# Token rows of the experts: indirect transfers through memory in place of one-hot products

## The reference

```python
logits = flat_x @ gate_w.T                        # 16 experts
scores = softmax(logits, axis=-1).T
topk_weight, topk_idx = top_k(scores, C)          # each expert takes its 74 best tokens
xg = flat_x[topk_idx]                             # [16, 74, 256]
g = einsum('ecd,eid->eci', xg, Wg)                # 1024 hidden
u = einsum('ecd,eid->eci', xg, Wu)
h = gelu(g) * u
eo = einsum('eci,edi->ecd', h, Wd) * topk_weight[..., None]
flat_out = zeros_like(flat_x).at[topk_idx.reshape(-1)].add(eo.reshape(-1, d))
out = flat_out + gelu(x @ Sg.T) * (x @ Su.T) @ Sd.T     # shared expert
```

## Time and profile before

| | |
|---|---|
| median of 3 runs | 814.61 us (814.48 to 814.78) |
| the profiled execution | 815.38 us, span 813.6 us |
| PE busy | 794.0 us, 98% |
| DVE busy | 632.2 us, 78% |
| ACT busy | 460.1 us, 57% |
| POOL busy | 251.7 us, 31% |
| moved by DMA | 88.36 MB, queue q1 busy 30.8% of 16 engines |

### The profile page before, as it was taken

The page is one execution under the profiler, slowest core; times in us unless marked ns, Lnnn a source line. Parts: engine busy times, 40 slices in busy tenths (PEclk is TensorE's granted clock), DMA queues, the critical chain, the costliest instruction groups (busy, mean ns, idle before and its releaser), DMA issues.

```text
span 813.6 us, 16629 instructions
## 1 busy us (share of the span) xinstructions
PE 794.0 (98%) x6060; PEld 744.2 (91%) x6060; DVE 632.2 (78%) x1287; ACT 460.1 (57%) x829; POOL 251.7 (31%) x297
## 2 busy tenths in 40 slices
PE   9999999999999999999999999999999999999988
PEld 8898789999999999898999999899998999999758
DVE  5796684778778776778797877878778787876796
ACT  3486424433333336585786778677687767745421
POOL 0012120410111100364366147336624623643020
PEclk9999999999999999999999999999999999999999
DMA  6010946998888822010210031031012103020001
GB/s 192 1 53 1 382 137 243 329 330 309 308 336 309 325 62 108 1 40 15 93 51 0 13 103 39 13 103 39 3 38 75 39 13 103 23 86 1 1 0 31
DMA packets 18290, 88.36 MB, mean 109 GB/s; under 512 B 3120, under 2 KB 7472, under 8 KB 12240
## 3 DMA queue, kind: packets, MB, share of 16 engines
q1 hardware_dynamic: 18256, 87.90, 30.8%
HBM read 85.05 MB, written 2.84 MB: 108 GB/s over the span
## 4 chain that ended last, share of the span: by engine, by line
PE 47%; issue 23%; POOL 18%; DVE 8%; ACT 3%; POOLq 0%; DVEq 0%; ACTq 0%
PE bank L1151 14%; POOL W_L L2017 7%; PE bank L1188 6%; POOL HF_L L2075 4%; POOL arena L1998 3%; PE bank L731 3%; POOL WQKV_L L2017 3%; PE bank L883 2%; PE bank L1197 2%; PE bank L1061 2%; PE bank L756 2%; PE bank L916 1%; PE bank L799 1%; POOL SQ L2036 1%; PE bank L1135 1%
## 5 line engine op out<-in xcount | busy, mean ns | idle before, releaser
L1151 PE MATMUL bank<-arena 128*128 (+1 forms) x1024 | 117.8, 274 | 0.0
L1151 PEld LDWEIGHTS bank<-arena 128*128 128x128 f32 x1024 | 117.4, 192 | 0.0
L1998 POOL TENSOR_TENSOR arena<-arena,srec 111x456 f32<-111x456 f32 x56 | 52.3, 961 | 123.8 <-DVE srec L2171 123.8
L2017 POOL TENSOR_TENSOR W_L<-LW,W_H 128x256 fp32r<-128x256 f32 x96 | 68.6, 751 | 35.4 <-DVE XHL L2609 32.1
L2075 POOL TENSOR_TENSOR HF_L<-arena,HF_H 128x296 fp32r<-128x296 f32 x48 | 43.8, 936 | 75.6 <-ACT HF_H L1913 75.6
L799 PE MATMUL bank<-XHL,W_H 128*128 128x296 f32 x288 | 64.8, 306 | 0.0
L1913 ACT ACTIVATE arena<-bank,vec 128x296 f32<-128x296 f32 x96 | 48.8, 509 | 20.8 <-PE bank L799 15.0
L2029 POOL TENSOR_TENSOR QW<-QW,arena x14 | 22.4, 1600 | 119.0 <-DVE QW L2510 65.6
L1342 PE MATMUL bank<-HF_L,W_H 128*128 128x296 f32 x192 | 57.4, 299 | 0.0
L1342 PE MATMUL bank<-HF_H,W_H 128*128 128x296 f32 x192 | 57.4, 299 | 0.0
L1342 PE MATMUL bank<-HF_H,W_L 128*128 128x296 f32 x192 | 57.3, 299 | 0.0
(11 more groups left out here) (276 smaller groups left out, 2183.4 us busy)
## 6 DMA issues: line engine op xcount, KB each, us to landing
arena<-ew_in SPq DMA_DIRECT2D x16, 2048.0 KB, 9.2
arena<-ew_in SPq DMA_DIRECT2D x16, 1024.0 KB, 6.9
LW<-lw_in SPq DMA_DIRECT2D x12, 1024.0 KB, 5.0
arena<-route SPq DMA_DIRECT2D x32, 185.0 KB, 3.3
LW<-lw_in SPq DMA_DIRECT2D x6, 768.0 KB, 4.4
fp_weights<-arena SPq DMA_DIRECT2D x1, 2048.0 KB, 6.4
arena<-fp_weights SPq DMA_DIRECT2D x1, 2048.0 KB, 7.3
arena<-patches_in SPq DMA_DIRECT2D x2, 864.0 KB, 8.3
```

What stands on the lines that cost most here:

```text
L1151: last = mm(o[:, m * CAP:(m + 1) * CAP], w[:, kc, mi * P:(mi + 1) * P], xg(kc, e), start=(kc == 0), stop=(kc == C - 1))
L1998: nc.gpsimd.tensor_tensor(v, v, srec[0:QROWS, s:s + 2, :].unsqueeze(3).to_broadcast([QROWS, 2, C * JH, KEYS]), ALU.mult).then_inc(p_ready, 1)
L2017: last = nc.gpsimd.tensor_tensor(low[:, cols], value[:, cols], high[:, cols], ALU.subtract)
```

## The change

Two tables in memory are new: `rows_in`, where SP stores the turned tokens together with their 16 scores (272 numbers a row), and `rows_out`, which POOL fills with zeros. Only experts 0 and 1 are still gathered by one-hot products, and only expert 15 is scattered by them. The rows of experts 0 and 1 are fetched by indirect transfers too, for their scores alone. Otherwise:

- DVE sums, for every slot, the numbers of the tokens in it (`expert_slots`) and turns them into integers. POOL fetches the 74 rows of `rows_in` by these numbers with an indirect transfer (`gather`), two experts ahead; PE turns them (`turn_gathered`, two transposes between down(e) and up(e+1)), and ACT copies them into one of two places in `XG`.
- DVE keeps token numbers and weights of the running expert (`keep_slots`), ACT scales its output (`EOT`), and POOL adds the 74 rows into `rows_out` by an indirect transfer that adds (`scatter`). Ahead of each indirect transfer POOL executes a one-element addition (`step`).
- At the end SP loads `rows_out`, and PE adds it into the banks by products with the identity (`add_rows`). The shared expert's result is added to `H` before the first expert.
- SP loads gate and up in transfers of their own (1 MB each), gate earlier than before, and one routing row in place of two.
- POOL's `split_weights("qkv", 0)` moves behind its loop.

```diff
-            def load_gate_up(e, s):
-                sp.dma_start(EW[s][:, 0:EGU_N], a["ew"][e][:, 0:EGU_N]).then_inc(ld_gu[s], 16)
+            def load_gate(e, s):
+                sp.dma_start(EW[s][:, 0:C * EI], a["ew"][e][:, 0:C * EI]).then_inc(ld_gu[s], 16)
+
+            def load_up(e, s):
+                sp.dma_start(EW[s][:, C * EI:EGU_N], a["ew"][e][:, C * EI:EGU_N]).then_inc(ld_up[s], 16)
...
+            by_tile = rows_in.rearrange("(t p) n -> p t n", p=P)
+            sp.wait_ge(moe_dve, MOE_DVE["probs"])
+            sp.dma_start(by_tile[:, :, D:GW], lg[:, 2]).then_inc(rows_stored, 16)
+            sp.wait_ge(moe_act, MOE_ACT["ut4"])
+            sp.dma_start(by_tile[:, :, 0:D], UT).then_inc(rows_stored, 16)
...
-            with sp.Fori(1, E // 2) as i:
+
+            def load_expert(i, s):
+
+                e2 = i * 4 + (2 * s - 4)
+                sp.wait_ge(u_psum, e2 + 2)
+                load_up(i * 2 + s, s)
+                sp.wait_ge(slot_summed, i * 2 + (s - 1))
+                load_route(i * 2 + s, s)
+                if not isinstance(i, int) or 2 * i + s < E - 1:
+                    sp.wait_ge(g_psum, e2 + 4)
+                    load_gate(i * 2 + (s + 1), 1 - s)
+                sp.wait_ge(d_psum, i * 2 + (s - 1))
+                load_down(i * 2 + s, s)
+
+            sp.wait_ge(g_psum, 2)
+            load_gate(2, 0)
+            with sp.Fori(1, E // 2 - 1) as i:
                 for s in range(2):
-
-
-                    sp.wait_ge(u_psum, i * 4 + (2 * s - 2))
-                    load_gate_up(i * 2 + s, s)
-                    sp.wait_ge(sw_ready, i * 2 + (s - 1))
-                    load_route(i * 2 + s, s)
-                    sp.wait_ge(d_psum, i * 2 + (s - 1))
-                    load_down(i * 2 + s, s)
+                    load_expert(i, s)
+            for s in range(2):
+                load_expert(E // 2 - 1, s)
+
+            sp.wait_ge(scattered, landed(E - 2))
+            sp.dma_start(TL, rows_out.rearrange("(t p) n -> p t n", p=P)).then_inc(ld_rows, 16)
...
-            for q in range(4):
-                pe.wait_ge(moe_dve, MOE_DVE[f"onehot{q}"])
-                for c in range(C):
-                    i = 2 * q + c
-                    if i >= 4:
-                        pe.wait_ge(moe_act, MOE_ACT[f"xg{i - 4}"])
-                    for t in range(NT):
-                        for part in (UT_H, UT_L):
-                            last = mm(bank[i % 4][:, 0:4 * CAP], part[:, t, c * P:(c + 1) * P],
-                                      OH[:, q % OH_RING, t, :, :].rearrange("p e s -> p (e s)"),
-                                      start=(t == 0 and part is UT_H), stop=(t == NT - 1 and part is UT_L))
-                    mark(last, f"xg{i}")
+            pe.wait_ge(moe_dve, MOE_DVE["onehot"])
+            for c in range(C):
+                for t in range(NT):
+                    for part in (UT_H, UT_L):
+                        last = mm(bank[2 + c][:, 0:2 * CAP], part[:, t, c * P:(c + 1) * P],
+                                  OH[:, t, :, :].rearrange("p e s -> p (e s)"),
+                                  start=(t == 0 and part is UT_H), stop=(t == NT - 1 and part is UT_L))
+                mark(last, f"xg{c}")
...
+            def turn_gathered(e, s):
+
+                if s == 0:
+                    pe.wait_ge(moe_dve, MOE_DVE["shared_added"])
+                pe.wait_ge(gathered[s], group(e) * 16 + 32)
+                pe.wait_ge(xg_ready, plus(e, 2))
+                for c in range(C):
+                    at = c * CAP
+                    last = nc.tensor.transpose(bank[5][:, at:at + CAP], G[0:CAP, s, c * P:(c + 1) * P], ident[0:CAP, 0:CAP])
+                last.then_inc(xg_turned, 1)
+
+            def add_rows():
+
+                pe.wait_ge(ld_rows, 16)
+                for c, t0, n, bk, col, opens in ACC:
+                    for t in range(NT):
+                        lo, hi = max(t0, t * P), min(t0 + n, (t + 1) * P)
+                        if lo < hi:
+                            mm(bank[bk][:, col + lo - t0:col + hi - t0], TL[:, t, c * P:(c + 1) * P],
+                               ident[:, lo - t * P:hi - t * P], start=(opens and lo == t0), stop=False,
+                               skip_group_check=True)
+
...
             def expert_step(e, s, nxt, ns):
 
-                if nxt is not None:
-                    gate_free(nxt)
-                    expert_up(nxt, ns, 0)
+                gate_free(nxt)
+                expert_up(nxt, ns, 0)
                 expert_down(e, s)
-                if nxt is not None:
-                    up_free(nxt)
-                    expert_up(nxt, ns, 1)
-                expert_scatter(e)
-
...
+            turn_weights(0, GROUPS_DOWN - 1)
+            add_rows()
+            turn_weights(GROUPS_DOWN - 1, GROUPS_DOWN)
+            last_scatter()
...
+            def expert_out(e1, s):
                 act.wait_ge(d_psum, e1 + 1)
-                act.wait_ge(sw_ready, e1 + 1)
-                if not (isinstance(e1, int) and e1 == 0):
-                    act.wait_ge(scat_done, e1)
-
-                f(EOT_H[0:CAP, :], bank[4][0:CAP, 0:D], ACT.Copy, scale=wslot[0:CAP, :]).then_inc(eot_ready, 1)
...
+            def gathered_out(e1, s):
+
+                act.wait_ge(xg_turned, e1 + 1)
+                f(XG[:, :, s, :], bank[5][:, 0:C * CAP].rearrange("p (c n) -> p c n", c=C), ACT.Copy
+                  ).then_inc(xg_ready, 1)
...
-            split_weights("qkv", 0)
+
+            def step(n):
+
+                if not (isinstance(n, int) and n == 0):
+                    pool.wait_ge(pool_stepped, n)
+                nc.gpsimd.tensor_tensor(pool_step[:, :], zero1[:, :], zero1[:, :], ALU.add).then_inc(pool_stepped, 1)
+
+            def gather(e, s, n):
+
+                pool.wait_ge(slot_ready, e + 1)
+                step(n)
+                pool.wait_ge(rows_stored, 32)
+                nc.gpsimd.indirect_dma_start(G[0:CAP, s, :], None, rows_in[:, :],
+                                             bass.IndirectOffsetOnAxis(ap=slot_id_i[0:CAP, s:s + 1], axis=0)
+                                             ).then_inc(gathered[s], 16)
+
+            def scatter(e, s, n):
+
+                pool.wait_ge(eot_ready, e + 1)
+                pool.wait_ge(scattered, landed(e, 0))
+                step(n)
+                pool.wait_ge(rows_stored, 32)
+                nc.gpsimd.indirect_dma_start(rows_out[:, :], bass.IndirectOffsetOnAxis(ap=scatter_id[0:CAP, s:s + 1], axis=0),
+                                             EOT[0:CAP, :], None, compute_op=ALU.add).then_inc(scattered, 16)
+
+            gather(0, 0, 0)
+            gather(1, 1, 1)
             with pool.Fori(0, QSLICES) as i:
-                for k, ready, done in ((1, w_scaled, w_divided), (0, w_rounded, w_quantised)):
+                for s, k, ready, done in ((0, 1, w_scaled, w_divided), (1, 0, w_rounded, w_quantised)):
+                    gather(i * 2 + (s + 2), s, i * 4 + (2 * s + 2))
+                    scatter(i * 2 + s, s, i * 4 + (2 * s + 3))
                     pool.wait_ge(ready, i + 1)
                     nc.gpsimd.tensor_tensor(QW_slice[:, i, :, :], QW_slice[:, i, :, :],
                                             qscale[:, i, k, :].unsqueeze(2).to_broadcast([P, QBLOCKS, FP4_BLOCK]),
                                             ALU.mult).then_inc(done, 1)
+
+            scatter(E - 2, 0, 4 * QSLICES + 2)
+            split_weights("qkv", 0)
...
-            def expert_weights(e1, group, s):
-
-
-                dve.wait_ge(ld_route[s], group * 32 + 32)
-                v.scalar_tensor_tensor(SW[0:CAP, :], PB[s][0:CAP, :], cst("iota_col")[0:CAP, :], WB[s][0:CAP, :],
-                                       ALU.is_equal, ALU.mult).then_inc(sw_full, 1)
-                dve.wait_ge(sw_full, e1 + 1)
-                v.tensor_reduce(wslot[0:CAP, :], SW[0:CAP, :], AX.X, ALU.add)
-                v.tensor_scalar(SHOT[0:CAP, :], PB[s][0:CAP, :], cst("iota_col")[0:CAP, :], None, ALU.is_equal
-                                ).then_inc(sw_ready, 1)
-
-            def split_output(e1):
-
-                dve.wait_ge(eot_ready, e1 + 1)
-                v.scalar_tensor_tensor(EOT_L[0:CAP, :], bank[4][0:CAP, 0:D], wslot[0:CAP, :], EOT_H[0:CAP, :],
+            def expert_slots(e, group, s):
+
+                dve.wait_ge(ld_route[s], group * 16 + 16)
+                v.scalar_tensor_tensor(SW[0:CAP, :], PB[s][0:CAP, :], cst("iota_col")[0:CAP, :], token_ids[0:CAP, :],
+                                       ALU.is_equal, ALU.mult, accum_out=slot_id[0:CAP, s:s + 1]).then_inc(slot_summed, 1)
+                dve.wait_ge(slot_summed, e + 1)
+                v.tensor_copy(slot_id_i[0:CAP, s:s + 1], slot_id[0:CAP, s:s + 1]).then_inc(slot_ready, 1)
+
+            def keep_slots(e, pair, s):
+
+                dve.wait_ge(gathered[s], pair * 16 + 16)
+                dve.wait_ge(scattered, landed(e, -1))
```

(8 more changed lines are left out.)

177 lines of the change are left out of this document (112 added, 65 removed).

## The result

The changed kernel takes 948.63 us (median of 5 runs, 947.26 to 953.99); the kernel before takes 814.61 us on the same chip. The ratio is 1.1653 [1.164, 1.1666], slower. Predicted were 920 us with a range of 858 to 972. The profiled execution has 953.99 us, span 952.0.

What follows compares the result with a forecast made beforehand. PE's work bounded the kernel before; after, a chain round the expert loop would. 14 steps of 18.8 us from a first marker at 126.5 give +102, the end +2.7, so about +105 on 815.4: 920 us, range 858 to 972.

Steps and rivals of the forecast that it cites:

- the forecast itself: A chain round the expert loop sets each step at 18.8 us: 920 us, own range 890 to 945, chance 0.52.
- rival 2: The expert loop's gather uses few of 16 DMA engines: step 22.1 us, time 966; chance 0.20.
- the 14 waits: Sign: PE waits at the transposes for a transfer or GpSimd about 14 times, 5 to 8 us each.
- PE's own saving and the first marker: Fewer gather products on PE: first marker, SP's start of an expert's weight load, at 126.5 us, 7.6 us sooner.
- SP's issue, the routing row, the slot table: From the marker: SP's issue 0.5 us, routing row landed at 5.8, DVE's slot table 1.2, reaching 7.0.
- The lock, 2.3 us: DVE's split of the down weights holds GpSimd's one-element add before the gather: 2.3 us, reaching 9.3.
- Issue and landing: Gather's issue on GpSimd 1.2 us, then its 80 KB landing 2.2 us, reaching 12.7 behind the marker.
- The clock, 1.5 us: TensorE's clock drops after PE's standstill, so the 32 up instructions take 1.5 us longer (0 to 2.1).
- The end: Behind the last step: last scatter and SP's load delay H's additions, +2.7 us; GpSimd's moved weight split costs nothing.
- Rival 1: Shorter chain: GpSimd's add slips ahead of DVE's split, clock stays up; step 15.0 us, time 866; chance 0.22.
- rival 3: Whole chain fits in PE's 6.35 us of gate and down: step 10.4, time 803; chance 0.03 with Rival 4.
- Rival 4: Change doesn't do what it says, gathers run an expert further ahead: 803 us; chance 0.03 with rival 3.

Runs made afterwards that it cites:

- run 2: SP asks for an expert's routing row before waiting for the up products, not behind the up load, against the changed kernel: 943.95 us.
- run 1: 26 constant products on PE ahead of each wait for a gather, against the changed kernel: 952.76 us.
- run 3: Gather fetches 80 rows instead of 74, DVE's slot table grown with it, against the changed kernel: 925.67 us.
- run 9: Routing row early, 80 slots per gather, and transposes inside the up products, against the changed kernel: 889.80 us.
- run 7: 80 slots per gather, and DVE waits for POOL's one-element add before the down-weights split, against the changed kernel: 926.72 us.
- run 12: As run 11, with the first encoder layer's output and feed-forward weights requested behind the last expert's weights: 827.68 us.
- run 11: Routing row early, 80 rows for gather and scatter, transposes inside up products, DVE's slot table ahead of rounding and split, against the changed kernel: 835.55 us.
- run 5: Transposes behind the up products, routing row requested before the up weights, and 80 slots per gather, against the changed kernel: 880.64 us.

## Why the prediction was right, and where it was off

The forecast's mechanism is what the trace shows: the transfer's chain round the loop sets the step, and PE waits for it at the transposes 14 times. The total is 29 us above the forecast: inside the range, but 3.6 us above the 890 to 945 that I gave the forecast itself, and so in the stretch of rival 2. Of the signs that I named, the 14 waits, the low clock and the first marker came. But 13 of the 14 waits are 1.2 to 3.8 us and not 5 to 8, and PE is busy for 84% of the stretch and not near 60%: more of PE's loss is slow products and less is standing still than I had it. By step:

- **PE's own saving and the first marker**: 127.25 against 126.5. Right.
- **SP's issue, the routing row, the slot table**: POOL's add at 7.0 us behind the marker, as summed. But run 2 shows that the row was nearly covered by DVE's share of the FP4 work, which I had left out of the chain, and that the gate load took back what an earlier gather won.
- **The lock, 2.3 us**: the mechanism was right, its occasion wrong. It shows in the first step only (2.10 us for the add); this is the step of the working that failed. In the 13 others the split is not ready, because ACT copies behind a gate that ran at the lower clock. I had taken the split as ready because the gate was fast. Runs 1, 3 and 9 show the lock of 2.1 us as soon as the gate is fast again. The earlier trace rows had priced it well. Run 7 adds that the transfer's instruction can be held as well as the add.
- **Issue and landing**: predicted 1.2 + 2.2 = 3.4 us, measured from the add's end at 7.2 to the landing at 13.5: 6.4. This is the term that was mis-sized, by 3.0. Run 3 takes it apart: in its fourteenth step, with 80 rows and no load just ahead, it is 3.1, and either the 74 rows or the gate load ahead brings some 2 us, both together 3. So rival 2's mechanism was at work beside the forecast's, but with 1.1 us of landing where a load stands ahead in any case (5.7 against 4.6), not 3.3; and that the gather would be issued just behind the gate load was in no term.
- **The clock, 1.5 us**: from the landing to the next marker I had 6.1 us and it took 7.2, +1.1. The whole gate and down run at the lower level too (85 us in all), but most of this lies in time in which PE would have waited. That is one reason why filling PE's wait in run 1 raised the clock and not the speed; the length of the fillers and the lock are the others.
- **Together**: lock -2.1 (the add ends at 7.2, not 9.3), issue and landing +3.0, clock +1.1 make +2.0; the step exceeds 18.8 by 1.9. It was luck that it is not more: the lock that did not come hid two thirds of the mis-sized transfer.
- **The end**: +2.7 us predicted behind the last step. Of the +18.2 us behind the last marker, the fourteenth step, which was in the sum, is 7.6 (up(14) ends at 415.3 us, 18.6 behind its marker). The other 10.6 are the end. The last scatter's instruction starts at 427.18 and SP can load its rows at 435.17, 8.0 us in place of the 4.0 summed; but that cost nothing, since the load landed 4.2 us later, at 439.4, and PE comes to its identity products at 440.54. What cost is a term that I had put at nothing: POOL's split of the qkv weights, moved behind its loop. It is early enough for PE, but it lies beside DVE's low part of the last hidden columns:

```profile
428.61 5.25 POOL L2105 TENSOR_TENSOR WQKV_L<-LW,WQKV_H 128x256 fp32r<-128x256 f32 x6
...
430.23 3.96 DVE L2639 TENSOR_TENSOR HH_L<-arena,HH_H 128x296 fp32r<-128x296 f32 x2
...
434.25 0.49 PE L1227 MATMUL bank<-EWD_H,HH_H 128*74 128x256 f32 x1 [4.51 <-DVE HH_L L2639]
```

The first of the two took 3.07 us, where the longest of the 32 in the kernel before took 0.47. PE stood still for 4.5 us and then ran down(15) at the lower clock, as it had gate(15) and most of down(14); the weight transposes start 23.8 us behind the fourteenth step in place of 14.4. This wait, 4.5 to 6.1 us, is in all twelve runs, run 12 included. That the split holds DVE is read from this overlap; no run moved it.

Rival 1 (no lock, clock up) fell on the clock; rival 3 (hidden) nearly came about in runs 11 and 12, with the scatter, the transposes and DVE's order changed as well, and there in some steps. Rival 4 fell with PE's 14 waits. Two slips in my working move nothing: the lower ends of the step add up to 10.9 with the hops, not 10.5, and the product of the earlier trace rows ended 1.1 us behind the split, not 1.3.

For the number of rows, 80 instead of 74 made gather and scatter faster (scatter issue 2.32 to 1.47 us). The Trainium skill's page "DMA: Bandwidth & Descriptors", section "Why a DMA increments its semaphore by 16 and not by 1", gives the largest divisor up to 16 as the number of engines, 2 for 74 and 16 for 80, and the DMA shares above agree for the indirect gather: about 2 engines of 16 with 74 rows, nearly 8 on the mean with 80. The same page of the Trainium skill has, in "Anatomy of one DMA — SWDGE (gpsimd) path", a fixed 2.0 us and bytes over 436 GB/s; the estimate of 2.2 us from it is near the shortest landings, 2.5 to 2.7 us with 80 rows and no load ahead, and under half of the 5.7 in the changed kernel. On the lock, the Trainium skill's page "SBUF — State Buffer", section "Who interferes with whom", says that DVE instructions of the split's kind (`tensor_tensor`) were not seen to stall a DMA; here the indirect one, whose row numbers are read from SBUF, went from 0.95 to 2.73 us beside it (run 7), and for this transfer the measurement decides.

What stays open: why the clock fell behind some waits of 1.2 us and not behind others (run 5); the price of the lock by itself, since each edit that took it away put a wait of the same size elsewhere; and what the best version would take with the qkv split in another place.

## What to carry to other kernels

When a transfer replaces PE work, follow the whole loop from the event that frees its first input to the engine that needs its last, and put each engine's other work in front of it: here the order on DVE (44 us) and loads queued ahead (8 us) decided whether it was hidden. A wait of PE can be paid a second time as clock in the step behind it, so a short wait left over is not always small. An edit that speeds up one engine brings other engines' work forward, and so can start the contention that it was free of. Work that is moved to where there is time for it can still hold up the engine beside it: look at who runs beside it, not only at when its result is wanted.
